# A graph attention kernel: the order of VectorE's work within one step

## The chip, the cores and the metric

One core of a Trainium2 chip runs the kernel; the other cores are idle. The metric is the device time of one execution in microseconds. Engines are named TensorE (PE in the rows, PEld for its weight loads), VectorE (DVE), ScalarE (ACT), GpSimd (POOL) and SyncE (SP), which issues DMAs.

## The reference

Eight graphs of 1024 nodes with 64 features each, and a dense 0/1 adjacency matrix per graph (int32, about 8 ones in a row of 1024). One layer of attention with 8 heads of 64 stands between a layer norm and a residual:

```python
h = jnp.maximum(_layernorm(x, axis=-1), 0.0)
q = (h @ Wq + bq).reshape(b, m, heads, d)          # k, v likewise
scores = einsum('bmhd,bnhd->bhmn', q, k) * scale + transpose(edge_bias[edges])
scores = leaky_relu(scores, 0.2)
scores = where(edges > 0, scores, -1e9)
out = einsum('bhmn,bnhd->bmhd', softmax(scores), v).reshape(b, m, heads * d)
x = x + out @ Wp + bp
```

## The kernel before

**Sparse keys.** The kernel doesn't compute 1024 x 1024 scores. A tile is 128 query rows; a graph has 8 tiles (TPG). The 128 queries of a tile are cut into 8 groups of 16 (GQ = 16). For each group and each block of 128 keys, the keys that some query of the group uses are ranked and packed into 32 slots (CAP), so that a group sees 8 x 32 = 256 slots (SLOTS). Scores are then 128 rows (8 heads x 16 queries) by 256 slots.

**One tile's way.** `convert` (GpSimd, L1032) turns the adjacency rows to bf16. TensorE turns them over (`turn_adj`, L1278) and counts per group which keys are used (`count`, L1287). VectorE reads the counts (`take_counts`), makes flags (`flag_used`), TensorE ranks the used keys with a triangular matmul (`rank`, L1294), VectorE takes the ranks (`take_ranks`, `val`) and marks one-hot matrices (`mark`, L1754). With these TensorE gathers keys and masks (L1233, L1247), ScalarE copies them out. The masks go through DRAM (`store_masks`, `spread_masks` on SyncE) to land as `mask_rows` beside the scores. The product side is folded: `q_hi` and `q_lo` are the two halves of a query projected with the folded weights, made by TensorE (L1369), ScalarE (`high_q`) and VectorE (`low_q`, L1716). The products of the edge bias come from `beta_done` (L1351) and are picked by VectorE in `pick_beta` (L1726, L1730).

**A pair.** Two groups are a pair, four pairs a tile, 32 pairs a graph. TensorE makes the scores of a pair in one bank (`scores`, L1207 and L1208). VectorE's `take_scores` (L1742) adds the mask, moves them to `w` and takes the row maximum `wmax`. From the maxima VectorE makes shifts for four groups at a time (L1799, L1806, L1816); GpSimd makes the other branch of the leaky unit, `a_line` (L1055, two instructions a pair, one behind another); VectorE takes the greater of the two (L1765, the first thing in its step). TensorE turns the result over (L1218), ScalarE takes the exponential, TensorE multiplies with the values (`weigh`, L1270), ScalarE copies out.

**A tile's end.** When four pairs are done, SyncE moves the tile's outputs into pairs of heads (`move_o`), and TensorE projects them in two halves (`project`, L1302, e = 0 and 1), both into the same bank. VectorE's `norm` divides a half by the softmax sums: for e = 0 it makes `den`, `alone` and `den_inv`, adds to `x_res` (L1849, both tensor operands in SBUF) and writes `o_all` (L1853); for e = 1 it only writes `o_all`. GpSimd's `add_heads` adds the heads up.

**The order.** Every engine runs the same numbered steps `s`, one pair a step, 32 a graph, and in a step it does what is due by a table of lags. The order inside a step is written out by hand for each engine; engines meet only at semaphores. Lags that matter here:

```python
LOAD, CONV, COUNT, TURN_A, USED, RANK, VAL, ONEHOT = 0, 4, 6, 5, 7, 8, 9, 9
MASK, MASK_OUT, MASK_IN, TFILL, QFILL, BETA, COLSUM, VEC = 10, 14, 15, 13, 9, 14, 18, 26
SCORE, A_LINE, Y, TURN, PV, X_ADD, MOVE_O, PROJ, NORM, SUM, OUT = 17, 19, 20, 21, 22, 24, 26, 31, 32, 34, 35
```

So `norm` of e = 0 is due in steps with s mod 4 = 0 and of e = 1 with s mod 4 = 1, together with `take_ranks`; `low_q` in even steps; `take_counts` and `flag_used` with s mod 4 = 3; `pick_beta` in steps 15 and 23 of each 32. In TensorE's step the order is scores, turn, weigh, gather keys, gather masks, natural copies, turn_adj, count, project, then the users of the bank `misc`: rank, edge products, q products and a few rare ones. Two of TensorE's banks are shared: `adj_bank` by turn_adj, count and both halves of project; `misc` by rank (`q_bank`), the edge products and the q products. Before each use TensorE waits until VectorE or ScalarE has read the last one:

```python
pe.wait_ge(used_ready, TPG * b + t + 1)      # rank
free(q_bank_uses, b, s, 0)                   # waits for low_q of the last q product
```

The scores have one bank, so TensorE's scores of a pair wait for `scores_taken` of the last pair.

Of the kernel before, what the change touches and what calls it, by code (L numbers as in the profile page):

```python
# [5 lines left out]
ALU = mybir.AluOpType  # L6
# [14 lines left out]
def preln_graph_attention(nc, x, adj, Wq, bq, Wk, bk, Wv, bv, edge_bias, Wp, bp, out):  # L21
# [8 lines left out]
    TPG = M // P  # L30
# [11 lines left out]
    LOAD, CONV, COUNT, TURN_A, USED, RANK, VAL, ONEHOT = 0, 4, 6, 5, 7, 8, 9, 9  # L42
# [11 lines left out]
    with ExitStack() as ctx, ExitStack() as prep, ExitStack() as fast:  # L54
# [223 lines left out]
        def pair(b, s, lag):  # L278
            p = s - lag
            return p if p >= 0 and not (isinstance(b, int) and b == B - 1 and p >= PPG) else None  # L280
# [5 lines left out]
        def tile(b, s, lag):  # L286
            return every(b, s, lag, 4)

        def piece(b, s, lag, count, stride=1):

            for f in range(count):
                t = tile(b, s, lag + stride * f)
                if t is not None:
                    return t, f
            return None
# [32 lines left out]
        def first(b, t):  # L328

            return b == 0 and t == 0  # L330
# [1303 lines left out]
        def _(dve):  # L1634
# [54 lines left out]
            def take_counts(b, t, src=adj_bank):  # L1689
                n = TPG * b + t  # L1690
                dve.wait_ge(cnt_done, n + 1)
                dve.nop(nofuse=True)
                nc.vector.tensor_tensor_reduce(cnt[:, t % 2, :], src[:, 0:TPG * GPT], zeros[:, :], 1.0, 0.0,
                                               ALU.add, ALU.add, cnt_sums[:, t % TPG:t % TPG + 1]).then_inc(cnt_ready, 1)
# [38 lines left out]
            def take_scores(b, p, u):  # L1733
                n, t, i = PPG * b + p, p // 4, slot(p, u)
                if u == 0:
                    if p % 4 == 0:
                        dve.wait_ge(mask_in[t % 2], 16 * H * (MT * b + t // 2 + 1))
                    if later(n, RING):
                        dve.wait_ge(y_turned, n - RING + 1)
                    dve.wait_ge(scores_ready, n + 1)  # L1740
                dve.nop(nofuse=True)
                nc.vector.tensor_tensor_reduce(w[:, i, :], row_bank[:, SLOTS * u:SLOTS * u + SLOTS],  # L1742
                                               mask_rows[:, t % 2, p % 4 * 2 + u, :], 0.25, LEAST_KEPT,
                                               ALU.add, ALU.max, wmax[:, i:i + 1]).then_inc(scores_taken, 1)
# [14 lines left out]
            def step(b, s):  # L1759
                p = pair(b, s, Y)  # L1760
                if p is not None:
                    for u in range(2):
                        i = slot(p, u)
                        dve.wait_ge(a_ready, 2 * PPG * b + 2 * p + u + 1)
                        nc.vector.scalar_tensor_tensor(w[:, i, :], w[:, i, :], shift[:, i:i + 1], a_line[:, i % 2, :],  # L1765
                                                       ALU.add, ALU.max).then_inc(y_ready, 1)
                t = tile(b, s, COUNT + 1)
                if t is not None and not first(b, t):
                    take_counts(b, t)
                p = pair(b, s, SCORE)  # L1770
                if p is not None:
                    for u in range(2):
                        take_scores(b, p, u)
                t = tile(b, s, USED)
                if t is not None and not first(b, t):
                    flag_used(b, t)
                    if t % TPG == TPG - 1:

                        dve.wait_ge(adj_copied, TPG * b + t + 1)
                        cols = square_sums_adj[:, bass.ds(TPG * b + t - TPG + 1, TPG)]  # L1780
                        nc.vector.tensor_tensor(cols, cols, cnt_sums[:, :], ALU.subtract).then_inc(kinds_noted, 1)
                due = piece(b, s, NORM, 2)
                if due is not None:
                    norm(b, *due)
                due = q_piece(b, s, QFILL + 1)
                if due is not None:
                    low_q(b, *due)
                t = tile(b, s, VAL)
                if t is not None and not first(b, t):
                    take_ranks(b, t)  # L1790
                four = p is not None and p % 2 == 1
                if four:
                    n = PPG // 2 * b + p // 2
                    cols = slice(slot(p - 1, 0), slot(p - 1, 0) + 4)
                    beta_four = beta[:, bass.ds(2 * PPG * b + 2 * p - 2, 4)]
                    if p % (PPG // 2) == 1:
                        dve.wait_ge(beta_ready, 2 * b + p // (PPG // 2) + 1)
                    dve.wait_ge(scores_taken, 2 * (PPG * b + p) + 2)
                    nc.vector.scalar_tensor_tensor(shift_neg[:, cols], wmax[:, cols], -5.0, beta_four,  # L1799
                                                   ALU.mult, ALU.subtract).then_inc(neg_ready, 1)  # L1800
                due = piece(b, s, ONEHOT, 4)
                if due is not None and not first(b, due[0]):
                    mark(b, *due)
                if four:
                    dve.wait_ge(neg_ready, n + 1)
                    nc.vector.scalar_tensor_tensor(shift[:, cols], wmax[:, cols], -1.0, shift_neg[:, cols],  # L1806
                                                   ALU.mult, ALU.min).then_inc(shift_ready, 1)
                if t is not None and t % TPG == TPG - 1:
                    dve.wait_ge(val_ready, TPG * b + t + 1)
                    nc.vector.tensor_tensor(val_top[:, :], val_top[:, :], val_max[:, :], ALU.max).then_inc(vals_noted, 1)  # L1810
                due = beta_piece(b, s, BETA + 1)
                if due is not None:
                    pick_beta(b, *due)
                if four:
                    dve.wait_ge(shift_ready, n + 1)
                    nc.vector.tensor_tensor(a_bias[:, cols], shift[:, cols], beta_four, ALU.add).then_inc(a_bias_ready, 1)  # L1816
                g = coming(b, s, CENTER)
                if g is not None:
                    center(g)
                g = coming(b, s, VARIANCE)  # L1820
                if g is not None:
                    variance(g)
                g = coming(b, s, NORMED)
                if g is not None:
                    normed(g)
                g = coming(b, s, LOW)
                if g is not None:
                    low(g)
                if isinstance(b, int) and b == B - 1:
                    flags(s)  # L1830

            def norm(b, t, e):
                n, heads = TPG * b + t, slice(4 * e, 4 * e + 4)
                dve.wait_ge(proj_done, 2 * n + e + 1)
                parts = adj_bank[:, 0:2 * P].rearrange("p (h d) -> p h d", d=D)
                if e == 0:
                    sums = adj_bank[:, 2 * P:2 * P + H]
                    nc.vector.tensor_scalar(den[:, :], sums, 1e-30, None, ALU.max).then_inc(den_ready, 1)  # L1838
                    nc.vector.tensor_scalar(alone[:, :], sums[:, 0:1], 0.5, None, ALU.is_lt).then_inc(alone_ready, 1)
                    dve.wait_ge(den_ready, n + 1)  # L1840
                    nc.vector.reciprocal(den_inv[:, :], den[:, :]).then_inc(den_inv_ready, 1)
                    dve.wait_ge(alone_ready, n + 1)
                    if t % TPG == 0:
                        dve.wait_ge(vec_ready, b + t // TPG + 1)
                    if t % MT == 0:
                        dve.wait_ge(x_added, 2 * b + t // MT + 1)
                    if later(n):
                        dve.wait_ge(summed, n)
                    nc.vector.scalar_tensor_tensor(x_res[:, t // MT % 2, t % MT, :], vecs[:, bass.ds(D * b + D * (t // TPG), D)], alone[:, :],  # L1849
                                                   x_res[:, t // MT % 2, t % MT, :], ALU.mult, ALU.add)\  # L1850
                        .then_inc(vec_added, 1)
                    dve.wait_ge(den_inv_ready, n + 1)
                nc.vector.tensor_tensor(o_all[:, heads, :], parts, den_inv[:, heads].unsqueeze(2).to_broadcast([P, 4, D]), ALU.mult)\  # L1853
                    .then_inc(proj_taken, 1)
# [98 lines left out]
```

## Time and profile before

| | |
|---|---|
| median of 3 runs | 998.11 us (997.89 to 999.87) |
| profiled execution, whole | 998.97 us |
| its span, first to last instruction | 997.2 us |
| TensorE busy | 943.0 us, 95% |
| VectorE busy | 902.0 us, 90% |
| ScalarE busy | 771.7 us, 77% |
| GpSimd busy | 518.9 us, 52% |
| mean granted TensorE clock | 0.987 of full speed |

The profile is of one execution. A busy time is the sum over an engine's instructions; register, branch and semaphore instructions are not counted. Waits are named by the engine and line that sat idle and by what came last before it went on; "issue" is time for which no releaser shows. Each engine's rows are in its own order, so a wait on one engine and the work that ends it stand in different rows.

### The profile page before, as it was taken

To read this page: it belongs to the slowest core of one execution; us is meant where nothing else is said; L and a number is where in the kernel's file an instruction comes from. 1 tells how busy PE (TensorE), PEld (TensorE's weight loads), DVE (VectorE), ACT (ScalarE), POOL (GpSimd) and SP (SyncE) were. 2 spreads that over 40 slices of the span, in tenths; PEclk is the share of its full clock that TensorE was granted. 3 is DMA by queue.
4 is the path that set the end of the run, shared out by engine and by line. 5 is a ranking of instruction groups with operands and counts; after the bars stand their busy time and mean duration, and the time that the engine had idled before them with its cause. 6 is when DMAs were issued, how large, how long until landed. Compare 5 with 4: busy or idle time off the path is not lost. (4 is left out here: it accounts for less than half of the span.)

```text
span 997.2 us, 28074 instructions
## 1 busy us (share of the span) xinstructions
PE 943.0 (95%) x8588; PEld 917.9 (92%) x8588; DVE 902.0 (90%) x3276; ACT 771.7 (77%) x1732; POOL 518.9 (52%) x956
## 2 busy tenths in 40 slices
PE   5889999999999999999999999999999999999995
PEld 4789999999999999999999999999999999999994
DVE  6699899998999999999999989999899998999983
ACT  5678887778787887787887788777878788778862
POOL 2144554745556555565556555474555655555454
PEclk9889999999999999999999999999999999999997
DMA  5424454545444555444554445444544455544431
GB/s 159 127 76 139 126 165 126 139 128 156 133 134 117 143 161 143 124 118 129 170 137 130 126 128 164 128 130 135 158 133 132 121 143 149 147 121 123 109 85 30
DMA packets 212661, 130.63 MB, mean 131 GB/s; under 512 B 38736, under 2 KB 203100, under 8 KB 212508
## 3 DMA queue, kind: packets, MB, share of 16 engines
q1 hardware_dynamic: 211716, 128.24, 47.0%
q8 instruction: 74, 1.21, 0.5%
q10 hardware_dynamic: 792, 0.53, 0.2%
q14 instruction: 79, 0.65, 0.2%
HBM read 71.83 MB, written 39.85 MB: 112 GB/s over the span
## 5 line engine op out<-in xcount | busy, mean ns | idle before, releaser
L1055 POOL TENSOR_SCALAR a_line<-w,a_bias 128x256 f32<-128x256 f32 x512 | 262.9, 513 | 414.4 <-DVE w L1765 369.6
L1270 PE MATMUL bank<-pt,nat_sb 128*65 128x128 f32 x2048 | 265.5, 273 | 0.3
L1526 ACT ACTIVATE pt<-bank 128x512 f32<-128x512 f32 x256 | 154.5, 603 | 114.1 <-PE bank L1218 107.7
L1742 DVE CUSTOM_DVE_ANT_0 w<-bank,mask_rows 128x256 f32<-128x256 f32 x512 | 195.4, 418 | 46.2 <-issue 37.2
L1765 DVE SCALAR_TENSOR_TENSOR w<-w,shift,a_line 128x256 f32<-128x256 f32 x512 | 230.4, 489 | 2.2 <-POOL a_line L1055 2.0
L1270 PEld LDWEIGHTS bank<-pt,nat_sb 128*65 128x65 f32 x2048 | 230.7, 138 | 0.8 <-issue 0.8
L1754 DVE TENSOR_TENSOR onehot<-val,counts_to 128x512 fp32r<-128x512 f32 x256 | 175.9, 687 | 2.2
L1508 ACT ACTIVATE mask_own<-bank,mask_bias 128x512 bf16<-128x512 f32 x256 | 176.7, 691 | 0.1
L1517 ACT ACTIVATE t_sb<-bank 128x512 fp32r<-128x512 f32 x256 | 152.0, 594 | 6.6 <-PE bank L1233 6.6
L1218 PE MATMUL bank<-ident,w 128*128 128x128 f32 x1024 | 153.8, 273 | 0.0
L1207 PE MATMUL bank<-t_sb,q_hi 128*128 128x256 f32 x512 | 143.3, 302 | 2.4 <-DVE wmax L1742 1.3
L1534 ACT ACTIVATE o_turned<-bank 65x256 f32<-65x256 f32 x256 | 99.1, 387 | 54.1 <-PE bank L1270 53.9
L1258 PEld LDWEIGHTS bank<-both_halves,t_sb 128*128 128x128 f32 x1024 | 137.4, 192 | 0.0
L1258 PE MATMUL bank<-both_halves,t_sb 128*128 128x64 f32 x1024 | 136.6, 257 | 0.0
L1208 PE MATMUL bank<-t_sb,q_lo 128*128 128x256 f32 x512 | 134.1, 284 | 0.0
L1043 POOL TENSOR_TENSOR o_all<-o_all 128x256 f32<-128x256 f32 (+2 forms) x192 | 121.8, 635 | 21.7 <-DVE o_all L1853 6.8
L1553 ACT ACTIVATE q_hi<-bank,q_bias 128x256 fp32r<-128x256 f32 x256 | 107.9, 478 | 23.7 <-PE bank L1369 23.6
L1716 DVE SCALAR_TENSOR_TENSOR q_lo<-bank,q_bias,q_hi 128x256 fp32r<-128x256 f32 x256 | 111.2, 474 | 15.8 <-ACT q_hi L1553 15.1
L1233 PE MATMUL bank<-onehot,h_nl 128*128 128x256 f32 x512 | 124.5, 325 | 0.0
L1218 PEld LDWEIGHTS bank<-ident,w 128*128 128x128 f32 x1024 | 118.7, 141 | 0.1
L1302 PE MATMUL bank<-w_pair,o_pairs 128*128 128x128 f32 x512 | 88.9, 297 | 18.6 <-DVE o_all L1853 17.3
L1247 PE MATMUL bank<-onehot,adj_t 128*128 128x256 f32 x512 | 104.9, 287 | 0.1
(137 smaller groups left out, 1620.5 us busy)
## 6 DMA issues: line engine op xcount, KB each, us to landing
adj_in<-in_adj_dram SPq DMA_DIRECT2D x64, 512.0 KB, 3.9
mask_store<-mask_own SPq DMA_DIRECT2D x64, 512.0 KB, 3.2
mask_rows<-mask_store SPq DMA_DIRECT2D x512, 64.0 KB, 2.4
o_pairs<-o_turned SPq DMA_DIRECT2D x128, 128.0 KB
stack_store<-h_stack SPq DMA_DIRECT2D x8, 512.0 KB, 3.6
x_rows<-in_x_dram SPq DMA_DIRECT2D x8, 256.0 KB, 5.2
x_res<-in_x_dram SPq DMA_DIRECT2D x16, 128.0 KB, 2.2
out_dram<-x_res SPq DMA_DIRECT2D x16, 128.0 KB, 2.1
```

The lines of the kernel that those rows point to most:

```text
L1055: nc.gpsimd.tensor_scalar(a_line[:, i % 2, :], w[:, i, :], 5.0, a_bias[:, i:i + 1], ALU.mult, ALU.add)\
L1207: pe.matmul(dst, q_hi[:, y % 2, GPT * (t % 2) + g, :], keys, start=True, stop=False)
L1208: last = pe.matmul(dst, q_lo[:, y % 2, GPT * (t % 2) + g, :], keys, start=False, stop=True)
L1218: last = pe.transpose(turned_bank[:, P * (2 * u + k):P * (2 * u + k) + P], w[:, slot(p, u), P * k:P * k + P], ident[:, :])
L1258: last = pe.matmul(nat_bank[:, D * (2 * u + k):D * (2 * u + k) + D], keys[:, P * k:P * k + P], both_halves[:, :], start=True, stop=True)
L1270: last = pe.matmul(o_part[0:D + 1, P * u:P * u + P], nat_sb[:, t % 2, p % 4 * 2 + u, k, :], pt[:, p % 2, u, k, :], start=(k == 0), stop=(k ...
L1508: nc.scalar.activation(mask_own[:, t % 2].rearrange("p g t j -> p t g j")[:, 2 * f:2 * f + 2], src[:, :].rearrange("p (t g j) -> p t g j", ...
L1517: nc.scalar.activation(t_sb[:, t % 2].rearrange("p g t j -> p t g j")[:, 2 * f:2 * f + 2], t_bank[:, :].rearrange("p (t g j) -> p t g j", ...
L1526: nc.scalar.activation(pt[:, p % 2], turned_bank[:, :].rearrange("p (u k r) -> p u k r", u=2, k=2), ACT.Exp, scale=0.8).then_inc(probs_rea ...
L1742: nc.vector.tensor_tensor_reduce(w[:, i, :], row_bank[:, SLOTS * u:SLOTS * u + SLOTS], mask_rows[:, t % 2, p % 4 * 2 + u, :], 0.25, LEAST_ ...
L1754: nc.vector.tensor_tensor(onehot[:, t % 2, 2 * f:2 * f + 2].rearrange("p t g j -> p (t g) j"), val[:, t % 2, cols * f:cols * f + cols].uns ...
L1765: nc.vector.scalar_tensor_tensor(w[:, i, :], w[:, i, :], shift[:, i:i + 1], a_line[:, i % 2, :], ALU.add, ALU.max).then_inc(y_ready, 1)
```

## The change

In VectorE's step, the norm of a half projection, the taking of ranks and the picking of edge products move ahead of the two `take_scores`; `low_q` moves ahead of `flag_used` (the two are never due in the same step). The subtraction in `square_sums_adj` stands outside the test for the very first tile. No instruction is added, removed or altered.

```diff
                 t = tile(b, s, COUNT + 1)
                 if t is not None and not first(b, t):
                     take_counts(b, t)
+
+                due = piece(b, s, NORM, 2)
+                if due is not None:
+                    norm(b, *due)
+                t = tile(b, s, VAL)
+                if t is not None and not first(b, t):
+                    take_ranks(b, t)
+                due = beta_piece(b, s, BETA + 1)
+                if due is not None:
+                    pick_beta(b, *due)
                 p = pair(b, s, SCORE)
                 if p is not None:
                     for u in range(2):
                         take_scores(b, p, u)
+                due = q_piece(b, s, QFILL + 1)
+                if due is not None:
+                    low_q(b, *due)
                 t = tile(b, s, USED)
                 if t is not None and not first(b, t):
                     flag_used(b, t)
-                    if t % TPG == TPG - 1:
...
-                due = piece(b, s, NORM, 2)
-                if due is not None:
-                    norm(b, *due)
-                due = q_piece(b, s, QFILL + 1)
-                if due is not None:
-                    low_q(b, *due)
+                if t is not None and t % TPG == TPG - 1:
...
                 t = tile(b, s, VAL)
-                if t is not None and not first(b, t):
-                    take_ranks(b, t)
                 four = p is not None and p % 2 == 1
...
-                due = beta_piece(b, s, BETA + 1)
-                if due is not None:
-                    pick_beta(b, *due)
                 if four:
```

## Rows read from the trace of the kernel before

**Rows 1.** The page, busy time, share and instructions of each engine.
```profile
PE 943.0 (95%) x8588; PEld 917.9 (92%) x8588; DVE 902.0 (90%) x3276; ACT 771.7 (77%) x1732; POOL 518.9 (52%) x956
```

**Rows 2.** List of waits: engine, line, releaser, us in total, times, longest.
```profile
DVE w L1742 <- issue: 37.2, 79, 1.3
...
PE bank L1302 <- DVE o_all L1853: 17.3, 27, 1.7
...
PEld bank L1294 <- issue: 14.6, 53, 2.3
```

**Rows 3.** Windows on TensorE's steps; busy (instructions) by engine, clock, DMA share, GB/s.
```profile
448.26:452.92 4.66, 3.60 (x32) 3.33 (x30) 4.66 (x16) 3.15 (x7) 2.07 (x3) 1.00 0.39 104
463.66:467.21 3.55, 3.45 (x32) 3.26 (x30) 2.81 (x14) 3.00 (x7) 1.91 (x3) 1.00 0.59 156
...
491.82:495.65 3.83, 3.60 (x31) 3.32 (x30) 3.38 (x14) 3.15 (x7) 2.07 (x3) 1.00 0.57 154
506.84:510.30 3.46, 3.45 (x32) 3.26 (x30) 3.46 (x16) 2.90 (x7) 2.12 (x3) 1.00 0.37 98
...
551.99:556.19 4.20, 3.60 (x32) 3.33 (x30) 3.43 (x13) 3.15 (x7) 2.21 (x4) 1.00 0.66 193
...
502.75:506.84 4.09, 4.00 (x34) 3.75 (x33) 4.02 (x14) 2.79 (x7) 1.51 (x4) 1.00 0.35 98
532.92:537.42 4.50, 4.00 (x34) 3.76 (x33) 4.43 (x15) 2.79 (x7) 3.65 (x10) 1.00 0.28 77
540.92:544.88 3.96, 3.83 (x36) 3.75 (x37) 3.89 (x15) 2.69 (x7) 2.13 (x6) 1.00 0.11 39
```

**Rows 4.** Timeline of TensorE, 446.5 to 453: start, duration, engine, line, [idle before].
```profile
447.15 0.69 PE L1302 MATMUL bank<-w_pair,o_pairs 128*128 128x128 f32 x4
447.68 0.27 PE L1305 MATMUL bank<-ident,den_rows 128*128 128x128 f32 x1
...
452.01 0.68 PE L1302 MATMUL bank<-w_pair,o_pairs 128*128 128x128 f32 x4 [0.96 <-DVE o_all L1853]
452.79 0.19 PE L1294 MATMUL bank<-used,lower 128*128 128x64 bf16 x1
```

**Rows 5.** Timeline of VectorE in the step at 448.26.
```profile
448.54 0.87 DVE L1765 SCALAR_TENSOR_TENSOR w<-w,shift,a_line 128x256 f32<-128x256 f32 x2
449.33 0.41 DVE L1742 CUSTOM_DVE_ANT_0 w<-bank,mask_rows 128x256 f32<-128x256 f32 x1
...
450.39 1.14 DVE L1849 SCALAR_TENSOR_TENSOR x_res<-vecs,alone,x_res 128x64 f32<-128x64 f32 x1
451.45 0.41 DVE L1853 TENSOR_TENSOR o_all<-bank,den_inv 128x256 f32<-128x256 f32 x1
451.79 0.86 DVE L1716 SCALAR_TENSOR_TENSOR q_lo<-bank,q_bias,q_hi 128x256 fp32r<-128x256 f32 x2
```

**Rows 6.** Timeline of GpSimd in the steps at 448.26 and 506.84.
```profile
449.21 1.12 POOL L1055 TENSOR_SCALAR a_line<-w,a_bias 128x256 f32<-128x256 f32 x2 [1.83 <-DVE w L1765]
450.42 1.04 POOL L1032 TENSOR_SCALAR adj_bf<-adj_in 128x1024 bf16<-128x1024 int32 x1
...
507.52 1.12 POOL L1055 TENSOR_SCALAR a_line<-w,a_bias 128x256 f32<-128x256 f32 x2 [2.61 <-DVE w L1765]
508.72 1.09 POOL L1032 TENSOR_SCALAR adj_bf<-adj_in 128x1024 bf16<-128x1024 int32 x1
```

**Rows 7.** Timeline of VectorE in the step at 506.84.
```profile
507.64 0.41 DVE L1742 CUSTOM_DVE_ANT_0 w<-bank,mask_rows 128x256 f32<-128x256 f32 x1
...
508.32 0.16 DVE L1838 TENSOR_SCALAR den<-bank 128x8 f32<-128x8 f32 x1
...
508.64 0.27 DVE L1849 SCALAR_TENSOR_TENSOR x_res<-vecs,alone,x_res 128x64 f32<-128x64 f32 x1
...
509.16 0.86 DVE L1716 SCALAR_TENSOR_TENSOR q_lo<-bank,q_bias,q_hi 128x256 fp32r<-128x256 f32 x2
```

More of the change, by code:

```diff
@@ L1776, in step @@
                     flag_used(b, t)
-                    if t % TPG == TPG - 1:
-                        dve.wait_ge(adj_copied, TPG * b + t + 1)
-                        cols = square_sums_adj[:, bass.ds(TPG * b + t - TPG + 1, TPG)]
-                        nc.vector.tensor_tensor(cols, cols, cnt_sums[:, :], ALU.subtract).then_inc(kinds_noted, 1)
-                due = piece(b, s, NORM, 2)
-                if due is not None:
-                    norm(b, *due)
-                due = q_piece(b, s, QFILL + 1)
-                if due is not None:
-                    low_q(b, *due)
+                if t is not None and t % TPG == TPG - 1:
+                    dve.wait_ge(adj_copied, TPG * b + t + 1)
+                    cols = square_sums_adj[:, bass.ds(TPG * b + t - TPG + 1, TPG)]
+                    nc.vector.tensor_tensor(cols, cols, cnt_sums[:, :], ALU.subtract).then_inc(kinds_noted, 1)
                 t = tile(b, s, VAL)
-                if t is not None and not first(b, t):
-                    take_ranks(b, t)
                 four = p is not None and p % 2 == 1
```

## Prediction

> **What bounds the kernel now.** I read the page's busy shares first [rows 1]: TensorE is busy 95% of the span, VectorE 90%. Two engines that close to full, passing tiles to each other, can only lose time in small waits between them, so the list of waits came next [rows 2]. Its entries for TensorE name VectorE: the second half projection (L1302) sits until VectorE's `o_all` has left the bank, and the rank matmul (L1294) sits some 0.3 us in 53 of 64 cases ("issue"). The opposite entry is VectorE's: before taking scores (L1742) it sat 37.2 us in 79 waits. TensorE waits for VectorE late in a step, VectorE waits for TensorE early in it.
>
> Then I cut one graph (32 steps, 448.26 to 566.53 us) into TensorE's steps, from one L1207 of a pair to the next [rows 3]. Only the steps with s mod 4 = 0 vary: 4.66, 3.55, 3.49, 3.83, 3.46, 4.26, 3.50 and 4.20 us, 30.95 together (five windows are shown, three left out: 3.49 at 477.96, 4.26 at 521.56, 3.50 at 537.42). I call them norm steps. A norm step without waits would take about 3.29: `project` starts 2.63 in, its matmuls take 0.53 (447.15 to 447.68), rank 0.13 (452.79 in [rows 4], window end 452.92 in [rows 3]).
>
> What ends a norm step last is one chain on VectorE: takes, norm, low_q. Rank needs the bank that low_q empties, and it stands in front of the next step's scores. In the step at 448.26 [rows 5] TensorE waits 0.96 us for `o_all` and then again for low_q [rows 4]; the next step begins 1.13 us after the first q_lo starts (451.79 to 452.92). Inside the chain sits an `x_res` of 1.14 us; in the step at 506.84 the same instruction takes 0.27 [rows 7]. The long one starts at 450.39 and lets `o_all` go at 451.45, just as GpSimd's adj_bf, 450.42 for 1.04 us, ends [rows 6]. So `x_res`, with two SBUF operands, waits out a GpSimd instruction.
>
> **The change part by part.** Nothing is added or removed, and no wait is new. The test around `kinds_noted` gives the same instruction at the same times: nothing. low_q and flag_used keep their place behind norm and takes: nothing. No DMA is issued by VectorE. SP's mask loads wait for takes, five steps earlier than the takes that need them; that is priced below.
>
> *Norm, first half.* Let d be the start of VectorE's step (L1765) less the start of TensorE's step. For the eight norm steps d is 0.28, -0.84, -0.90, -0.55, 0.01, -0.12, 0.01, -0.96 (the first is 448.54 in [rows 5] less 448.26). Now takes start at the later of d + 0.79 (448.54 to 449.33 in [rows 5]) and 0.77, when the scores are there. Afterwards norm fills that wait, its input (the first projection, in TensorE's step before) being ready. Norm, from `den` to q_lo, is 0.84 (508.32 to 509.16 in [rows 7]). What changes is the neighbour on GpSimd: `x_res` is issued at start + 0.79 + 0.32 = 1.11 us (0.32 is 508.32 to 508.64 in [rows 7]), when GpSimd is in the first instruction of a_line. That pair began 0.67 after the start (448.54 and 449.21 in [rows 5, 6]) and runs 1.12, so its first ends at about 1.22: a wait of 0.11, of which I charge 0.08 over the 0.84. The convert that cost up to 0.9 comes later and is passed. Takes then begin at d + 1.71, q_lo after another 0.69 (takes, 507.64 to 508.32 in [rows 7]), the next TensorE step 1.13 later. New length: the later of d + 3.53 and 3.29.
>
> By that, the eight go to 3.81, 3.29, 3.29, 3.29, 3.54, 3.41, 3.54, 3.29: 27.46, or 3.49 less. Where a wait of 0.2 to 0.8 us before takes, or a stall of `x_res`, existed it is gone; where d is about 0 with no stall, nothing is won.
>
> The Trainium skill (SBUF — State Buffer, "SBUF: two separate sides") says that VectorE with two SBUF inputs and a GpSimd instruction that reads SBUF exclude each other for the whole of whichever began first. The trace agrees in [rows 5, 6]. [...]
>
> *Norm, second half, and ranks (s mod 4 = 1).* They put 0.34 + 0.28 us ahead of takes. Takes end about d + 2.1 there, with d at most 1.0, and TensorE's step is 3.69: covered. One step gains: at 540.92 [rows 3] TensorE takes 3.96 instead of 3.69, waiting for the second `o_all` before it turns adj; with norm first that wait goes: 0.3 less.
>
> *Edge products (steps 15 and 23 of a graph, 502.75 and 532.92 in [rows 3]).* TensorE waits for `beta_pick` before its q matmuls, and for little else. They take 4.09 and 4.50; without the wait 3.74. But takes now stand 1.38 us (the two instructions of pick_beta) later: at d = 0.29 they end at 3.5, covered; at d = 0.64 they end near 3.8 and hold the next scores to 3.93. So 0.35 and 0.57 less. VectorE has the same work in these steps and comes no earlier, so d of the following norm steps rises by the same amounts and their lengths too (3.54 to 3.89 and 4.11): plus 0.92. The edge products are worth nothing; VectorE is the bound over those two steps.
>
> Sum per graph: -3.49 - 0.3 - 0.92 + 0.92 = -3.8 us. Six graphs are like that: -22.8. The seventh (803.41 to 919.67) has no long convert collision in three of its norm steps (3.42 to 3.43): -2.2. Four norm steps remain behind it (3.86, 3.41, 3.56, 3.02): -0.9. I give back 1 us for small waits that appear in a faster loop. Together -25. The profiled execution took 998.97 (span 997.2, 1.8 around it), so it would be 974; the median shown is 998.11, 0.9 lower: **973 us**.
>
> What is late next: in most norm steps TensorE itself (3.29); in four of eight still low_q. The mask loads: the last of eight issues starts 2.9 to 5.8 us before its takes and lands after 2.4 (median), so at the tightest 0.5 is left, and four steps get up to 0.9 shorter while takes move 0.6 later. Where this fails it costs 0.3 once or twice a graph, 2 to 4 us in all.
>
> **The rivals.**
> *A: as above.* For it: the lengths of all norm steps now follow from d and the stall of `x_res` within 0.05.
> *B: `x_res` waits out the whole pair of a_line.* GpSimd goes from one to the next in 0.1 us. Then the wait is to start + 1.79, 0.65 us instead of 0.08 in each norm step. Carried through the steps, a graph gains 1.2 instead of 3.8: about 990 us. Against: at 508.64 `x_res` begins exactly when the second a_line ends, and the convert issued at 508.72 runs 1.09, not 1.04: VectorE got in between two waiting GpSimd instructions [rows 6, 7].
> *C: slower: GpSimd holds on through both a_lines and the convert.* The three now lie back to back right behind L1765, so `x_res` would wait until start + 2.9, 1.6 us more in each norm step, where today it mostly meets the tail of the convert. A graph would be 6 to 7 us longer, 1040 us. It turns to a loss from a stall of 0.8 us per norm step on. Against: the same rows as for B. For it: nothing shown, but no row has a request in just this place.
> *D: nothing comes of it.* Rank waits for low_q, which stays behind the same sum of work; where VectorE has no wait before takes, only the order changes. This would hold if the waits before takes were not in the norm steps: 996 to 999. Against: the differences between the eight windows with the same work [rows 3].
>
> **How the numbers follow.** A has 0.78 with 967 to 981 of its own: below if the floor is 3.2 rather than 3.29 and `x_res` waits nothing (6 us), above if the masks are late or half of the norm steps meet a longer stall. B 0.11, C 0.05, D 0.06. The range reaches from 967 toward B, to 986, leaving B's centre, C and D out. 0.2% (2 us) is about what can be told from no change. Faster: A, B and part of D, 0.90; same 0.04; slower 0.06.
>
> **What would show it.** The wait of L1302 for `o_all`, 17.3 us, falls under 3; that of L1369 for `beta_pick` goes, and a wait of L1207 for `wmax` appears at one step in 32. VectorE's "issue" wait before L1742 falls by two thirds in norm steps. `x_res` stays under 0.5 us everywhere and a_line or the convert right after it grows a little. Graph windows shrink from 118.3 to about 114.5 us, the first and second norm step of a graph to some 3.8 and 3.3. It would be wrong if `x_res` still showed a second form of 0.6 us or more, if TensorE's steps with s mod 4 = 1 grew beyond 3.7, or if takes waited for `mask_rows`.

## The result, and the profile after

The changed kernel takes 966.38 us (965.65 to 970.47) beside 998.09 for the kernel before on the same chips: a ratio of 0.9683, 95% interval 0.966 to 0.9706. The profiled execution took 965.85 us with a span of 964.1. It is faster, as forecast, but by 31.7 us where 25 were forecast, and the median lies 0.6 us below the range (by the interval of the ratio, 964.2 to 968.7 us).

The busy times of the page, beside [rows 1]:

```profile
PE 925.8 (96%) x8588; PEld 913.6 (95%) x8588; DVE 875.1 (91%) x3276; ACT 769.7 (80%) x1732; POOL 514.9 (53%) x956
```

VectorE's busy time fell from 902.0 to 875.1 us with the same 3276 instructions: some of what counted as busy had been waiting. The 64 `x_res` alone, 37.2 us together before and 16.4 after, are 20.8 of these 26.9 us. The list of waits, beside [rows 2]:

```profile
DVE w L1742 <- issue: 29.7, 43, 1.3
...
PEld bank L1294 <- issue: 13.4, 22, 2.7
...
PE bank L1294 <- DVE q_lo L1716: 10.0, 22, 2.6
...
PE bank L1302 <- DVE o_all L1855: 4.4, 3, 2.0
```

L1302 waited 17.3 us in 27 places for `o_all`, now 4.4 in 3, all three behind 946 us, where the last tiles run out. The weight load of rank (L1294) sat in 53 places, now in 22, but longer in each. The wait for `beta_pick` is gone. VectorE's waits before the first L1742 of a step, added up from the timeline over the whole run, were 24.7 us in 35 norm steps and 16.1 in steps with s mod 4 = 2; they are 1.8 in two norm steps and 31.4 in steps with s mod 4 = 2. VectorE's slack now lies two steps later, and TensorE's steps there are as long as before (the first two of the graph below 3.23 and 3.25 us, before 3.24 and 3.23).

TensorE's steps, cut as in [rows 3], same graph and same order (seven of the eight norm steps, then the two pick steps, and the step behind the norm step of 4.00):

```profile
433.80:437.59 3.79, 3.44 (x31) 3.25 (x30) 3.79 (x16) 3.14 (x7) 2.07 (x3) 1.00 0.47 128
448.34:451.53 3.19, 3.19 (x31) 3.18 (x30) 3.15 (x16) 2.63 (x6) 1.89 (x3) 1.00 0.44 128
475.83:479.01 3.18, 3.18 (x31) 3.17 (x30) 3.18 (x15) 2.63 (x6) 2.08 (x3) 1.00 0.49 139
489.83:493.57 3.74, 3.44 (x32) 3.25 (x30) 3.74 (x16) 3.14 (x7) 2.07 (x3) 1.00 0.39 105
504.84:508.12 3.28, 3.28 (x31) 3.25 (x30) 3.28 (x15) 2.73 (x6) 2.07 (x3) 1.00 0.50 120
519.02:523.02 4.00, 3.56 (x31) 3.37 (x30) 4.00 (x16) 3.14 (x7) 2.67 (x5) 1.00 0.65 192
533.84:537.02 3.18, 3.18 (x32) 3.17 (x30) 3.18 (x14) 2.63 (x6) 2.36 (x5) 1.00 0.61 164
486.11:489.83 3.72, 3.72 (x34) 3.72 (x33) 3.65 (x14) 2.79 (x7) 1.18 (x3) 1.00 0.32 94
515.23:519.02 3.79, 3.79 (x34) 3.68 (x32) 3.72 (x15) 2.77 (x7) 3.02 (x10) 1.00 0.32 93
523.02:526.73 3.71, 3.71 (x38) 3.71 (x38) 3.68 (x15) 2.25 (x6) 1.97 (x5) 1.00 0.02 7
```

In the steps of 3.18 TensorE is busy throughout: nothing is left to wait for. In the norm steps of 3.74 to 4.00 it is VectorE (third busy column) that is busy throughout: there VectorE is the bound. In the step of 3.28, in the two pick steps (the steps with `pick_beta`) and in the last one shown both are busy nearly throughout. With the one left out (3.18) the eight norm steps are 27.54 us, before 30.95. The whole graph:

```profile
448.26:566.53 118.27, 114.84 (x1067) 112.18 (x1065) 111.09 (x405) 94.96 (x214) 65.16 (x119) 1.00 0.50 137
```

is the kernel before, and after it is

```profile
433.80:547.37 113.57, 112.48 (x1066) 111.55 (x1065) 107.60 (x405) 94.73 (x214) 64.94 (x119) 1.00 0.53 143
```

The timeline of VectorE in the first norm step of that graph, beside [rows 5]:

```profile
434.08 0.87 DVE L1765 SCALAR_TENSOR_TENSOR w<-w,shift,a_line 128x256 f32<-128x256 f32 x2
434.87 0.15 DVE L1840 TENSOR_SCALAR den<-bank 128x8 f32<-128x8 f32 x1
...
435.23 0.28 DVE L1851 SCALAR_TENSOR_TENSOR x_res<-vecs,alone,x_res 128x64 f32<-128x64 f32 x1
435.43 0.42 DVE L1855 TENSOR_TENSOR o_all<-bank,den_inv 128x256 f32<-128x256 f32 x1
435.77 0.41 DVE L1742 CUSTOM_DVE_ANT_0 w<-bank,mask_rows 128x256 f32<-128x256 f32 x1
...
436.45 0.87 DVE L1716 SCALAR_TENSOR_TENSOR q_lo<-bank,q_bias,q_hi 128x256 fp32r<-128x256 f32 x2
```

and GpSimd's, beside [rows 6]:

```profile
434.74 1.12 POOL L1055 TENSOR_SCALAR a_line<-w,a_bias 128x256 f32<-128x256 f32 x2 [1.83 <-DVE w L1765]
435.95 1.04 POOL L1032 TENSOR_SCALAR adj_bf<-adj_in 128x1024 bf16<-128x1024 int32 x1
```

`x_res` took 1.14 us here and takes 0.28. It is over before the convert (435.95) begins, and between the two a_lines it gets in at once: in 53 of the 64 tiles it begins 0.06 to 0.12 us before the first a_line ends, and it takes 0.24 to 0.28 us there. Over all 64 tiles, minimum, median and maximum before and after:

```profile
L1849 DVE SCALAR_TENSOR_TENSOR x_res<-vecs,alone,x_res x64: 243/364/1151, 95.1 to 988.3; 128x64 f32<-128x64 f32 x64
```

```profile
L1851 DVE SCALAR_TENSOR_TENSOR x_res<-vecs,alone,x_res x64: 242/245/350, 94.2 to 954.4; 128x64 f32<-128x64 f32 x64
```

### The profile page after: what moved, and what is told of

It reads as the page before. It is cut to its first block and busy times, and to the rows that moved or that the text cites. A ratio compares the mean times of both kernels' runs of the same rounds, so it can differ in the third digit from the quotient of the medians.

```text
span 964.1 us, 28074 instructions
## 1 busy us (share of the span) xinstructions
PE 925.8 (96%) x8588; PEld 913.6 (95%) x8588; DVE 875.1 (91%) x3276; ACT 769.7 (80%) x1732; POOL 514.9 (53%) x956
## 5 line engine op out<-in xcount | busy, mean ns | idle before, releaser
L1742 DVE CUSTOM_DVE_ANT_0 w<-bank,mask_rows 128x256 f32<-128x256 f32 x512 | 195.3, 418 | 39.5 <-issue 29.7
L1765 DVE SCALAR_TENSOR_TENSOR w<-w,shift,a_line 128x256 f32<-128x256 f32 x512 | 228.3, 485 | 2.2 <-POOL a_line L1055 2.0
L1207 PE MATMUL bank<-t_sb,q_hi 128*128 128x256 f32 x512 | 144.1, 303 | 1.7 <-DVE wmax L1742 1.2
L1043 POOL TENSOR_TENSOR o_all<-o_all 128x256 f32<-128x256 f32 (+2 forms) x192 | 114.3, 595 | 21.7 <-DVE o_all L1855 6.8
L1207 PEld LDWEIGHTS bank<-t_sb,q_hi 128*128 128x128 f32 x512 | 97.4, 190 | 4.9 <-DVE wmax L1742 1.7
```

Source lines behind the costliest of these rows:

```text
L1207: pe.matmul(dst, q_hi[:, y % 2, GPT * (t % 2) + g, :], keys, start=True, stop=False)
```

## The experiments

All times are medians, each ratio is against the kernel before on the same chip with its 95% interval. "Graph" is the length of the same graph, from the first L1207 of its first norm step (118.27 before, 113.57 after).

| kernel | us | ratio | graph, us |
|---|---|---|---|
| norm alone moved | 968.32 | 0.9688 (0.966 to 0.9716) | 113.90 |
| edge products alone | 998.33 | 0.9994 (0.9979 to 1.0008) | 118.31 |
| ranks alone | 998.01 | 0.998 (0.9965 to 0.9994) | 118.24 |
| before, `x_res` behind low_q | 985.15 | 0.9855 (0.9827 to 0.9883) | 116.37 |
| after, `x_res` behind takes | 986.12 | 0.9871 (0.9844 to 0.9899) | 116.67 |
| before, convert first on GpSimd | 992.38 | 0.9939 (0.9918 to 0.9961) | 117.27 |
| after, second half of norm back | 970.71 | 0.9722 (0.9702 to 0.9741) | 114.02 |
| after, sum of edge products twice | 982.61 | 0.9825 (0.9789 to 0.9861) | 115.17 |
| after, that sum two steps later | 960.76 | 0.9627 (0.9602 to 0.9653) | 113.01 |
| and low two steps later | 957.79 | 0.9586 (0.9557 to 0.9615) | 112.42 |
| and center six steps earlier | 955.36 | 0.9568 (0.9549 to 0.9586) | 112.32 |

### The three moves one by one

Each is the kernel before with one block ahead of the takes:

```diff
+                due = piece(b, s, NORM, 2)
+                if due is not None:
+                    norm(b, *due)
                 p = pair(b, s, SCORE)
```

> The kernel before with only norm (both halves) ahead of take_scores; ranks and edge products stay where they were. Theory 1 (VectorE's queue: norm fills the wait for the scores, and x_res leaves the convert behind it; the moved edge products only shift time from the pick step to the norm step behind it): the same as the changed kernel within 2 us, 965 to 969 us. Theory 2 (the three moves each add their part; TensorE waited 7.9 us for beta_pick in 15 waits): 972 to 976 us.

```diff
+                due = beta_piece(b, s, BETA + 1)
+                if due is not None:
+                    pick_beta(b, *due)
                 p = pair(b, s, SCORE)
```

> The kernel before with only pick_beta ahead of take_scores. Theory 1: TensorE's steps 15 and 23 of a graph shrink by 0.4 and 0.7 us, the norm steps 16 and 24 behind them grow by as much: 996 to 999 us. Theory 2: the wait for beta_pick is gone and not paid back: 989 to 992 us.

```diff
+                t = tile(b, s, VAL)
+                if t is not None and not first(b, t):
+                    take_ranks(b, t)
                 p = pair(b, s, SCORE)
```

> The kernel before with only take_ranks ahead of take_scores. Theory 1: the second o_all now stands behind ranks and takes and is 0.28 us later, so turning adj (L1278) waits about 0.15 us in each step with s mod 4 = 1: up to 8 us slower, 1002 to 1007. Theory 2: nothing or a small gain, 995 to 998.

Norm alone gives 968.32 us, all but some 2 us of the change. The edge products alone give nothing: their two steps fall from 4.09 and 4.50 to 3.73 and 3.91 us, and the norm steps behind them grow from 3.46 and 3.50 to 3.80 and 4.08. That is theory 1, and theory 2, that each move adds its part, falls: the wait for `beta_pick` could be removed without gaining anything.

For ranks I was wrong: no 8 us of loss. The step at 540.92 grows, from 3.96 to 4.17, and the others with s mod 4 = 1 by 0.05; but the norm steps and the second pick step shrink by as much (for example 4.66 to 4.61, 4.50 to 4.35), because VectorE's own work takes no longer and a longer TensorE step leaves it less late in the next. The graph is unchanged. It is the same balance as with the edge products, with the other sign.

### What x_res waits for

In the first kernel `x_res` leaves `norm` and is issued behind low_q; the order is that of the kernel before otherwise.

```diff
                 due = q_piece(b, s, QFILL + 1)
                 if due is not None:
                     low_q(b, *due)
+                due = piece(b, s, NORM, 2)
+                if due is not None:
+                    add_alone(b, *due)      # x_res += alone * vecs, first half only
```

> The kernel before in its own order, but x_res (L1849) of the first half goes behind low_q, so that its wait for GpSimd's convert stands in front of nothing that TensorE waits for. Theory 1: the collision is the larger part of the gain: 3.5 us a graph, 972 to 977 us, norm steps 3.2 to 3.5 us. Theory 3 (the wait for scores that norm fills is the larger part, the collision a small one): 985 to 992 us.

It took 985.15: at the edge of theory 3, 8 us above the upper end of theory 1. The stalls ahead of low_q are indeed gone: the eight norm steps are 3.45 or 3.46 us but for the first two, 3.84 and 3.53. Two things eat the rest. Taking `x_res` out saves only its stall, not its own 0.19 (508.64 to 508.83): `o_all` needs `den_inv`, and it started 0.49 after `den` here, where it was 0.51 with `x_res` in between (508.32 to 508.83 before):

```profile
441.19 0.15 DVE L1841 TENSOR_SCALAR den<-bank 128x8 f32<-128x8 f32 x1
...
441.68 0.42 DVE L1848 TENSOR_TENSOR o_all<-bank,den_inv 128x256 f32<-128x256 f32 x1
```

And behind low_q it makes VectorE 0.19 later in each next step (d 0.78 instead of 0.59), where the second `o_all` is then late: 3.80 instead of 3.69 in most. So what this kernel gains, 1.9 of the 4.7 us a graph, is a net: the norm steps lose 2.85 (30.95 to 28.10), the steps behind them grow by 0.78 and three others by 0.17 together. Neither theory holds as it was worded. The length of the norm steps came out as theory 1 had it, but for two, and the 3.5 us a graph did not; the time is that of theory 3, but the collision is no small part, since norm alone takes 4.09 us off the norm steps (30.95 to 26.86) and this kernel 2.85.

The second puts it the other way: the changed kernel, with `x_res` back behind the takes.

```diff
                 if p is not None:
                     for u in range(2):
                         take_scores(b, p, u)
+                due = piece(b, s, NORM, 2)
+                if due is not None:
+                    add_alone(b, *due)
```

> The changed kernel, but x_res (L1849 of before) goes back behind take_scores, ahead of low_q; den, den_inv and o_all stay in front. Theory 1 (low_q's place in VectorE's queue decides, and what x_res meets there): x_res is issued about 2.3 us after the start of VectorE's step, inside the convert (1.9 to 2.9), waits about 0.6, and norm steps with d over -0.8 grow by as much: 3 us a graph, 984 to 989 us. Theory 4 (TensorE's wait of L1302 for o_all was what mattered, and o_all still leaves the bank early): as the changed kernel, 965 to 969.

986.12 us, 3.1 us a graph lost. VectorE, GpSimd and TensorE in the first norm step:

```profile
443.70 0.87 DVE L1765 SCALAR_TENSOR_TENSOR w<-w,shift,a_line 128x256 f32<-128x256 f32 x2
...
444.99 0.42 DVE L1850 TENSOR_TENSOR o_all<-bank,den_inv 128x256 f32<-128x256 f32 x1
446.01 0.68 DVE L1861 SCALAR_TENSOR_TENSOR x_res<-vecs,alone,x_res 128x64 f32<-128x64 f32 x1
446.62 0.86 DVE L1716 SCALAR_TENSOR_TENSOR q_lo<-bank,q_bias,q_hi 128x256 fp32r<-128x256 f32 x2
```

```profile
445.58 1.04 POOL L1032 TENSOR_SCALAR adj_bf<-adj_in 128x1024 bf16<-128x1024 int32 x1
```

```profile
445.98 0.69 PE L1302 MATMUL bank<-w_pair,o_pairs 128*128 128x128 f32 x4
447.63 0.19 PE L1294 MATMUL bank<-used,lower 128*128 128x64 bf16 x1 [0.95 <-DVE q_lo L1716]
```

`x_res` is issued at 446.01, the convert runs until 446.62, `x_res` ends 0.07 us behind it, and low_q begins at 446.62. The second projection did not wait at all; the 0.95 us stand before rank. So theory 4 falls: the early release of the bank is not what gives the most of the change. What counts is when low_q is through. Of the 4.7 us a graph 1.6 are left here (118.27 to 116.67); what part of them comes from the early `o_all`, from the filled wait or from the other moves was not taken apart. The share of the collision depends on the order in which it is taken: 1.9 net when it goes first, 3.1 when it comes back last.

Its mirror on the other engine leaves VectorE's order of before and puts the convert ahead of the lines:

```diff
             def step(b, s):                     # GpSimd
+                t = tile(b, s, CONV)
+                if t is not None:
+                    convert(b, t)
                 p = pair(b, s, A_LINE)
...
-                t = tile(b, s, CONV)
-                if t is not None:
-                    convert(b, t)
```

> The kernel before, VectorE's order untouched; in GpSimd's step the convert goes ahead of a_line. x_res is then issued when GpSimd is idle. Theory 1: x_res 0.24 us everywhere, the long norm steps (4.66, 4.26, 4.20, 3.83) fall to 3.45 to 3.75: 2.0 to 2.9 us a graph, unless the convert now meets mark in the step before; 978 to 986 us, and the wait for scores stays to be won. Theory 4: L1302 still waits for o_all behind takes, only shorter: the same number, but a change of VectorE's order would be needed to get below 990.

992.38: less gain than in either theory. `x_res` mostly no longer waits (median 0.246), but the convert finds other victims. One is `low` in the step before, which has two SBUF operands too and takes 1.52 us instead of 0.68:

```profile
444.51 1.52 DVE L1658 TENSOR_TENSOR h_nl<-x_rows,h_nl 128x512 fp32r<-128x512 f32 x1
```

```profile
444.04 1.46 POOL L1032 TENSOR_SCALAR adj_bf<-adj_in 128x1024 bf16<-128x1024 int32 x1
```

The convert itself takes 1.46 instead of 1.04, since it starts while `mark` (443.91, 0.68) runs. The first norm step stays at 4.63 us, because VectorE comes to it 1.11 us late. The seventh grows from 3.50 to 4.22; there the greater of the two lines (L1765) is hit, 1.59 us instead of 0.87:

```profile
533.34 1.59 DVE L1765 SCALAR_TENSOR_TENSOR w<-w,shift,a_line 128x256 f32<-128x256 f32 x2
```

```profile
533.21 1.05 POOL L1032 TENSOR_SCALAR adj_bf<-adj_in 128x1024 bf16<-128x1024 int32 x1
```

The third grows from 3.49 to 3.94, where `x_res` (476.20) meets another instruction of GpSimd, L1097 (476.16 for 0.73), and takes 0.77.

### The second half of norm

```diff
                 due = piece(b, s, NORM, 2)
-                if due is not None:
+                if due is not None and due[1] == 0:
                     norm(b, *due)
...                                             # behind take_scores
+                if due is not None and due[1] == 1:
+                    norm(b, *due)
```

> The changed kernel with the second half of norm (e = 1) back behind take_scores; ranks stay in front. Theory 1: the second o_all is late for turn_adj only where d is near 0.6 or more; 0.05 us in some steps and 0.4 in step 25: 968 to 971 us. Theory 4 (the early release of the bank matters in each tile): 0.2 us in each of 64 tiles, 976 to 980.

970.71 us, 0.45 us a graph: as theory 1 says. In the step behind the seventh norm step (4.18 us, 3.70 in the changed kernel) TensorE waits for it again:

```profile
525.88 0.61 PE L1278 MATMUL bank<-ident_bf,adj_bf 128*128 128x128 bf16 x8 [0.33 <-DVE o_all L1858]
```

### Is VectorE the bound of the long norm steps?

First more work in the pick steps, then less. The sum of `pick_beta` is done twice, once into a spare tile:

```diff
+                nc.vector.tensor_reduce(spare[:, :], beta_pick[:, half], AX_X, ALU.add).then_inc(spare_done, 1)
+                dve.wait_ge(spare_done, 2 * n + half + 1)
                 dve.wait_ge(beta_picked, 2 * n + half + 1)
                 nc.vector.tensor_reduce(beta[...], beta_pick[:, half], AX_X, ALU.add).then_inc(beta_ready, 1)
```

> The changed kernel with the sum of pick_beta done once more, into a spare tile, in steps 15 and 23 of a graph (0.6 to 0.7 us more VectorE work in each). Theory 1: VectorE has no slack over those steps and the norm step behind each; 0.7 us twice a graph come out whole, shared between the step itself (scores wait for takes) and the next: 1.3 to 1.5 us a graph, 975 to 978 us. Theory 5 (TensorE at 96% busy is the bound there too): under half of it, 966 to 970.

The graph grows by 1.60 us (113.57 to 115.17), a little more than two such sums (0.72 each, from the start of one to the start of the next): the pick steps go from 3.72 and 3.79 to 4.25 and 4.53, the norm step behind the first from 3.74 to 4.02. The median, 982.61, is higher than seven such graphs explain. In the profiled execution that is the start, not the change: between 43 and 93 us the granted clock was 0.79 in the mean here and 0.86 in the profile of the changed kernel, and the first graph starts 5.6 us later (98.88, 93.25). The fourth execution, with a mean clock of 0.988 against 0.979 or 0.98 in the other three, took 977.13 us, within theory 1.

Then the sum two steps later:

```diff
+                due = beta_piece(b, s, BETA + 3)
+                if due is not None:
+                    sum_beta(b, *due)           # the tensor_reduce of pick_beta, at the step's end
                 g = coming(b, s, CENTER)
```

> The changed kernel with pick_beta cut in two: the product that empties the bank stays in steps 15 and 23 of a graph, the sum over it (L1730 of before, 0.69 us) moves two steps on, to the end of steps 17 and 25, where VectorE has time before the scores. Theory 1 (VectorE's lateness d in a norm step is the bound of the long ones): d of steps 16 and 24 falls by 0.6, their lengths 3.73 and 4.00 to 3.18 and 3.4, 1.1 us a graph, 957 to 960 us. Theory 5 (at 96% busy TensorE has nothing left to give, the waits turn up elsewhere): 964 to 967.

960.76 us, 0.56 a graph where 1.1 was expected. The step behind the first pick falls to 3.18, the one behind the second to 3.61; but step 20 of the graph grows from 3.28 to 3.57, since the deferred sum and `center` in step 19 now make VectorE late there, and the first norm step from 3.79 to 3.90. About half of the gain is handed on. Theory 5, nothing left for TensorE to gain, falls. The next two diffs show only the lags that matter of a longer line.

```diff
-NORMED, HIGH, LOW, TURN_H = 29, 30, 31, 34
+NORMED, HIGH, LOW, TURN_H = 29, 30, 33, 34
```

> The same, and low (L1658, 0.68 us once a graph) goes from step 31 to step 33, out of the step before the first norm step. Theory 1: d of the first norm step falls from 0.28 to -0.3, its length from 3.79 to 3.18: another 0.6 us in six graphs, 953 to 957 us. Theory 5: 964 to 967.

957.79 us, 0.8 above the range of theory 1. The first norm step goes to 3.29 us where 3.18 was expected. Last, with that too:

```diff
-X_LOAD, CENTER, SQUARES = 8, 19, 20
+X_LOAD, CENTER, SQUARES = 8, 13, 20
```

> The kernel with the sum of pick_beta and low moved (defer_low), and center (L1637, L1639, 1.3 us once a graph) from step 19 to step 13, where VectorE waits 1.6 us for the scores of the next step. Theory 1: d of norm step 20 falls from 0.12 under -0.25, its length from 3.55 to 3.18: 0.37 us a graph in six graphs, 955 to 957 us against 957.8. Theory 5: no difference, 957 to 959.

955.36 us, the fastest here: 11 us under the changed kernel. Step 20 falls from 3.52 to 3.18 and step 24 from 3.60 to 3.36, but step 16, right behind the new place, rises from 3.19 to 3.65. Against the kernel ahead of it the gain is 2.4 us in the medians but only 0.1 in this graph and at most 0.2 in others (0.8 in all seven), so most of those 2.4 are not shown to be its own.

## Why the prediction was right and where it was not

The mechanism and the direction were right; the size was not. Two terms of the sum failed, each for some 0.4 us a graph: the floor of a norm step, put at 3.29 us and measured at 3.18, and VectorE's chain in the steps that it ends, put at d + 3.53 and measured at d + 3.42, with 0.08 us in it for a wait of `x_res` that mostly did not occur.

*What bounds it, and the direction: right.* VectorE's chain to low_q ends a norm step; norm alone gives nearly all of the gain, and with the early `o_all` but `x_res` late only 1.6 of the 4.7 us a graph remain. The collision of `x_res` with the convert is a part of it.

*The collision gets short: right, and charged too high.* I charged 0.08 us per norm step behind the first a_line. Mostly there was none: `x_res` took 0.245 in the median. With the rest of the chain also somewhat shorter than summed, a norm step that VectorE ends takes d + 3.42 rather than d + 3.53 (0.58 and 4.00; -0.14 and 3.28); only the first and the fifth of the graph, where `x_res` takes 0.28, lie higher (0.28 and 3.79, 0.29 and 3.74). In the four norm steps that VectorE ends this is 0.02 + 0.15 + 0.13 + 0.11 = 0.41 us a graph.

This is the lock that the Trainium skill describes (SBUF — State Buffer, "SBUF: two separate sides"): of a VectorE instruction with two SBUF inputs and a GpSimd instruction that reads SBUF, the one that starts first holds the shared ports to its end, and the other waits. The runs agree in both directions. In the kernel before, `x_res` ended 0.07 to 0.09 us behind the convert in all 42 tiles where it met one, and `low` grew from 0.68 to 1.52 us when the convert was put in its way; there the convert, started during `mark`, grew from 1.04 to 1.46.

*The floor of a norm step, 3.29 us: wrong, and by a little the largest single miss.* I added project's 0.53 and rank's 0.13. The 0.13 was read behind a wait. Where rank doesn't wait, its weights load while project still runs, and the next scores start 0.03 after it. TensorE in the second norm step after the change:

```profile
450.98 0.69 PE L1302 MATMUL bank<-w_pair,o_pairs 128*128 128x128 f32 x4
451.50 0.19 PE L1294 MATMUL bank<-used,lower 128*128 128x64 bf16 x1
451.53 0.36 PE L1207 MATMUL bank<-t_sb,q_hi 128*128 128x256 f32 x1
```

```profile
451.39 0.10 PEld L1294 LDWEIGHTS bank<-used,lower 128*128 128x128 bf16 x1
```

The floor is 3.18, in four norm steps of eight: 0.42 us a graph.

*The pick steps: right in kind.* They lose 1.08 us rather than 0.92, since the second reaches 3.79 rather than 3.93. That what they gain is paid back behind them held: alone, they are worth nothing. Within the changed kernel they and the ranks bring the 0.3 us a graph by which it beats norm alone; which of the two does was not taken apart.

*The second half of norm: 0.25 us forecast as 0.3*, and 0.45 when it is put back.

*The sum.* The graph was forecast to lose 3.8 us and lost 4.70; the difference is 0.41 + 0.42 + 0.16 - 0.05, less another 0.04 in the steps where nothing was forecast. Six graphs (from 93.3 to 803.41 before, 93.25 to 774.50 after) lost 28.8 instead of 22.8, the seventh (803.41 to 919.67, now 774.50 to 887.52) 3.2 instead of 2.2, the four norm steps behind it 1.4 instead of 0.9. The 1 us that I gave back for new small waits wasn't needed. So the mechanism was right and its size short by a quarter: nearly every term that I rounded, I rounded towards less gain, and the range below carried only 6 us for all of them together.

*The rivals.* B (waiting out both a_lines) and C (and the convert) did not occur: 0.350 us is the longest `x_res`. D did not either. The masks stayed just in time; the list of waits has 2.4 us for `mask_rows` in two places, before 2.1 in one.

*The signs.* Most came as named. Four did not: L1302 still waits 4.4 us for `o_all`, not under 3, though only at the run's end; L1207 waits for `wmax` in two places of the run, not in one step of 32; VectorE's wait before the takes went almost wholly out of the norm steps, not by two thirds; and neither a_line nor the convert behind `x_res` grew (median of the convert 1.046 and 1.045 us).

## What to carry to other kernels

Where two engines are both nearly full, write down per step how late one is against the other, and ask of each moved instruction which step's end it sits in front of; a wait that vanishes between two steps bound by the same engine (here the edge products) can be paid back in the next. An instruction that is moved also meets other neighbours: the same 64-element add cost 0.24 or 1.15 us depending on which GpSimd instruction ran beside it, and moving the neighbour instead changed who was hit. A duration read behind a wait is not the one that the same work has in a stream without waits, so a floor should be read from a stretch that runs without them, or else kept as the upper bound.

## What the runs showed of the hardware that I had not expected

- The rank matmul, of 64 columns, between two others costs 0.13 us until the next when it has just been released (452.79 to 452.92 before), and 0.03 when it had not to wait (451.50 to 451.53 after).
- VectorE gets in between two GpSimd instructions that stand 0.1 us apart: no `x_res` of the changed kernel took over 0.350 us, where waiting for the second a_line would have taken it to some 0.7 (an estimate: 0.1 to the end of the first, 0.1 between the two, 0.48 for the second).
- The start of a run varies with the granted clock: its mean was 0.79 of full speed between 43 and 93 us in one profile and 0.86 in three others, and the first graph began at 98.88 us instead of 93.25.
